# Pacing of embedding gathers: scratch writes between gathers replaced by an answered semaphore

## The reference

```python
h = relu(dense @ dw1 + db1)                      # 512 x 13 -> 512 x 64
dense_emb = relu(h @ dw2 + db2)                  # 512 x 64
sparse_emb = emb_tables[f_ids, sparse_idx]       # 512 x 26 x 64, tables 26 x 12500 x 64
emb = concatenate([dense_emb[:, None, :], sparse_emb], axis=1)
inter = einsum('bfd,bgd->bfg', emb, emb)         # 27 x 27 products per sample
pairs = inter[:, iu0, iu1]                       # the 351 above the diagonal
z = concatenate([emb.reshape(B, -1), pairs], axis=1)
z = relu(z @ ow1 + ob1)                          # 2079 -> 512
z = relu(z @ ow2 + ob2)                          # 512 -> 256
z = relu(z @ ow3 + ob3)                          # 256 -> 128
return z @ ow4 + ob4                             # 128 -> 1
```

## Time and profile before

| | |
|---|---|
| median of the runs | 188.66 us |
| the profiled execution, whole | 187.21 us |
| its span, first to last instruction | 185.4 us |
| TensorE busy, mean granted clock | 127.4 us (69%), 0.88 |
| GpSimd busy | 123.8 us (67%) |
| ScalarE, VectorE busy | 42.2 us, 37.8 us |
| gathers on GpSimd | 104, 98.9 us busy |
| scratch writes on GpSimd | 90, 24.7 us busy |

### The profile page before, as it was taken

How to read it: one execution, slowest core, us unless ns; L and a number is a source line. 1 busy time by engine, 2 the same in 40 slices (tenths; PEclk the granted TensorE clock), 3 DMA queues, 4 the chain that set the end, 5 groups by cost and what they waited for, 6 DMA issues and landing times.

```text
span 185.4 us, 3069 instructions
## 1 busy us (share of the span) xinstructions
PE 127.4 (69%) x1301; PEld 68.8 (37%) x1301; DVE 37.8 (20%) x97; ACT 42.2 (23%) x96; POOL 123.8 (67%) x199
## 2 busy tenths in 40 slices
PE   1510285828655995839439993959729979989994
PEld 0000132514344442524226432424426446656453
DVE  2700003000142204100144005000234023136011
ACT  0440310031046201040075001040174011166011
POOL 3888888888735888888565888888367887200000
PEclk9999999975965699996965798587997999999999
DMA  5999532221212332312312332222222324100000
GB/s 157 409 332 357 172 26 23 23 28 21 21 13 23 21 22 24 28 22 26 24 13 24 23 27 20 23 28 20 19 20 20 22 25 31 18 4 0 4 0 0
DMA packets 4576, 9.80 MB, mean 53 GB/s; under 512 B 2065, under 2 KB 2065, under 8 KB 3922
## 3 DMA queue, kind: packets, MB, share of 16 engines
q0 software_dynamic: 3328, 3.41, 21.3%
q1 hardware_dynamic: 1010, 5.30, 7.1%
q10 hardware_dynamic: 224, 0.89, 1.6%
HBM read 9.59 MB, written 0.00 MB: 52 GB/s over the span
## 4 chain that ended last, share of the span: by engine, by line
PE 45%; POOL 26%; issue 18%; ACT 5%; DMA 3%; DVE 2%
PE acc L259 20%; POOL gathered L211 20%; PE acc L292 10%; PE inter L276 7%; POOL pace L219 6%; PE acc L310 4%; DMA gathered<-tables,rows 2%; ACT emb L386 1%; ACT emb L387 1%; PE turned L240 1%; PE acc L301 1%; ACT pairs L392 1%; DMA idx_raw<-idx 1%; ACT z L399 1%; DVE emb L466 1%
## 5 line engine op out<-in xcount | busy, mean ns | idle before, releaser
L211 POOL DMA_INDIRECT gathered<-tables,rows x104 | 98.9, 951 | 34.6 <-issue 16.9
L259 PE MATMUL acc<-w,emb 128*128 128x512 f32 x104 | 65.7, 780 | 19.4 <-issue 12.3
L259 PEld LDWEIGHTS acc<-w,emb 128*128 128x128 f32 x104 | 31.3, 315 | 46.3 <-issue 36.9
L392 ACT ACTIVATE pairs<-inter 28x96 f32<-28x96 f32 (+1 forms) x64 | 15.7, 246 | 39.8 <-PE inter L276 39.1
L219 POOL MEMSET pace<- 128x192 uint8 x90 | 24.7, 274 | 0.1
L292 PE MATMUL acc<-w,pairs 128*128 128x512 f32 x56 | 24.7, 592 | 0.0
L182 DVE COPY pairs<-inter 28x96 f32<-28x96 f32 (+1 forms) x64 | 17.0, 266 | 26.5 <-PE inter L276 25.8
L276 PE MATMUL inter<-emb 64*28 64x28 f32 x1024 | 12.6, 204 | 13.8 <-DMA gathered<-tables,rows 10.1
L240 PE MATMUL turned<-small,gathered 128*128 128x128 f32 x52 | 10.1, 317 | 13.5 <-DMA gathered<-tables,rows 13.5
L386 ACT ACTIVATE emb<-turned 128x512 f32<-128x512 f32 x8 | 8.8, 1098 | 45.7 <-issue 28.6
L465 DVE COPY emb<-turned 128x512 f32<-128x512 f32 (+1 forms) x7 | 5.5, 784 | 64.1 <-issue 49.5
(11 more groups left out here) (47 smaller groups left out, 26.3 us busy)
## 6 DMA issues: line engine op xcount, KB each, us to landing
w<-w SPq DMA_DIRECT2D x5, 1024.0 KB, 8.7
gathered<-tables,rows POOLq DMA_INDIRECT x104, 3.4
small<-small_pack ACTq DMA_DIRECT2D x1, 706.5 KB, 6.0
dense_sb<-dense_pack ACTq DMA_DIRECT2D x1, 160.5 KB
idx_raw<-idx SPq DMA_DIRECT2D x1, 39.0 KB
idx_raw<-idx SPq DMA_DIRECT2D x1, 13.0 KB, 1.9
out<-y SPq DMA_DIRECT2D x1, 2.0 KB
```

The source lines that it names most:

```text
L211: pool.indirect_dma_start(out=gathered[:, t, s, :], out_offset=None, in_=tables, in_offset=bass.IndirectOffsetOnAxis(ap=rows[:, t, s:s + 1 ...
L259: nc.tensor.matmul(acc[t][:], emb[:, tile_of(t), place(2 * c)], w[:, c, :], start=(c == 0), stop=False)
L392: last = move(lambda dst, src: nc.scalar.activation(dst, src, ACT.Copy), t, k, (0, 1))
```

## The change

The scratch buffer and its writes are gone. Every gather now increments `gathers_issued`. SyncE waits for each gather's increment in turn and increments `echo` once (ECHOES = 1). GpSimd issues gather n = 26 t + s only when `echo` shows the answer to gather n - 2 (LAG = 2). The holds stay where they were, and TensorE waits for the same gathers as before, now counted on `gathers_issued`.

```diff
-PACE = 192
+ECHOES = 1
+LAG = 2
 HOLDS = [7, 10]
-UNPACED_FROM = 18
...
-        pace = sb("pace", [P, TILES * NF, PACE], mybir.dt.uint8)
...
-        gathers_held = sem("gathers_held")
+        gathers_issued = sem("gathers_issued")
+        echo = sem("echo")
...
                 sp.dma_start(w[:, groups, :], w1[:, groups, :]).then_inc(w_in[g], 16)
+            for n in range(TILES * NF - LAG):
+                sp.wait_ge(gathers_issued, n + 1)
+                for _ in range(ECHOES):
+                    sp.sem_inc(echo, 1)
             sp.wait_ge(y_done, 2)
...
                     for s in range(2 * c0, 2 * c1):
-                        held = t > 0 and s in HOLDS
+                        n = t * NF + s
+                        if n >= LAG:
+                            pool.wait_ge(echo, ECHOES * (n - LAG + 1))
                         pool.indirect_dma_start(
...
-                            engine_sem=gathers_held if held else None,
+                            engine_sem=gathers_issued,
                         ).then_inc(group_in[t][g], 16)
-                        if held:
+                        if t and s in HOLDS:
                             pool.wait_ge(inter_done, 2 * (t - 1) + HOLDS.index(s) + 1)
-                        elif t < LAST or s < UNPACED_FROM:
-                            nc.gpsimd.memset(pace[:, t * NF + s, :], 0)
...
                 if t < LAST:
-                    pe.wait_ge(gathers_held, 2 * t + k + 1)
+                    pe.wait_ge(gathers_issued, (t + 1) * NF + HOLDS[k] + 1)
```

## The result

The changed kernel took 221.67 us in the median of four runs (220.51 to 222.16), the kernel before 188.63 us (187.79 to 189.02). The ratio is 1.175, with a 95% interval of 1.169 to 1.181. I had forecast 183.1 us and a gain.

A forecast was written before the change was run, and what follows sets the result against it. Neither TensorE (69% busy) nor GpSimd (67%) was the bound by share; TensorE waited for gathers in places. Gains of 3.1, 0.28, 1.7, 0.28 and 0.28 made 5.6 us: 183.1 us against the 188.66 median, range 180.0 to 190.0.

The forecast's parts named there:

- My list of what would prove me wrong: Pitch above 1.35 us, gathers longer than 0.95, landings after 3.7, or TensorE's products lengthening by over 1.3 us a group.
- the clock: TensorE's granted clock: fewer waits may win or lose half-clock groups; taken as 0, with 2.5 us on each side.
- At most 3.7: Reading of the trace before: a gather takes 3.4 us from start to landing, at most 3.7.
- later than 3.7 us: Sign of being wrong: gathers that land later than 3.7 us after their start.
- Rival C: Every gather: the 0.27 us release adds to each 0.30 us gap, pitch 1.52, kernel slower at 199.1 us; chance 0.16.
- First tile: Up to interactions(0, 0): gathers come sooner, TensorE waits less, and its start moves from 50.62 to 47.5, 3.1 us.
- Hold: Hold of tile 1: the three gathers inside have two pitches of 0.14 us less, a gain of 0.28 us.
- Tile 1 with its hold: Tile 1: TensorE's waits of 0.81 and 0.88 us go, 1.7 us; the hold of tile 2 gives 0.28.
- Tile 2 with its hold: Tile 2: TensorE is already the later engine, GpSimd 1.1 us early, gain 0; the hold of tile 3 gives 0.28.
- Last tile: Last tile: field 25 already has 2.2 us of slack before turn(3, 3), so gain 0.
- case A: Whole kernel: the gain comes as summed, 183.1 us, own range 180.6 to 185.6; chance 0.60, 0.04 more for a gain beyond.

## Why the prediction was wrong

**The number failed on the chip of the result, and the step that failed was the one I didn't write as a step.** In the sum I let each copy start right behind its turn, as in the trace before, and counted only what gathers do to TensorE's waits for data. On that chip the increments behind four turns took 6 to 11 us, and one behind layer 2's products 4.3 us: 37 us of added waits where the sum had nothing. My list of what would prove me wrong has the pitch, the length of a gather, the landing and the clock, and not this. I took the trace of one execution as the behaviour of the kernel.

**One reading was too narrow as well.** "At most 3.7" for the landing covers only the 24 gathers whose landings were all recorded, each within eight gathers behind a hold. On chip 14, where all 104 are recorded, the same view gives, before and with the change:

```profile
DMA to landing us min/median/max: 2.3/3.3/7.3
DMA to landing us min/median/max: 2.3/3.3/6.9
```

The long ones are the first eleven gathers of tile 0 (4.2 to 7.3 us before), which run beside the weight loads. The median holds, so the sum doesn't change, but "later than 3.7 us" was no sign of being wrong.

**Rival C** had the right sign and the wrong mechanism. The wait is free. The pitch stays 1.25 us from the second gather to the 34th, so it was not the queue of GpSimd either. The Trainium skill, Advanced Engine Details and Errata, Engine Queue Depths, gives that queue eight places; in this trace nothing changes past the eighth gather. The warning of rival C, that only eight gathers in a row had been seen without a write, was right in one respect. What goes wrong in the result comes with long runs of them: turn(1, 1) and turn(2, 1), about 13 us into a run of gathers, are followed by copies that are 0.3 and 0.9 us late, and the four that are late by 6 us and more come over 20 us into one. The order isn't strict: turn(0, 0), which ends 17 us into the first run, is followed by its copy at once (20.74, 20.78).

**What is shown and what is not.** Shown: the changed kernel is 17.5% slower in the result's runs and about 5% faster on three chips. The difference is made by TensorE's increments, which reach the engines that wait for them up to 10.8 us late. On the chips of the experiments neither pitch, nor answers, nor about twice the increments makes it appear. Not shown: what is different about the result's chip, and whether the pitch or the answers do the harm there, since no variant ran on it. There are signs that something on it was busy before the change too. The kernel before was 2% slower there. Its landing events were incomplete in the trace. In its first interactions TensorE stood still twice, for 0.59 us before 51.69 and for 0.52 before 52.39, where on chip 14 the same 128 matmuls run through in 1.26 us:

```profile
51.69 0.18 PE L276 MATMUL inter<-emb 64*28 64x28 f32 x1 [0.59 <-issue]
```

One explanation that fits is a path for recorded events that is slow there, which gathers at 1.25 us fill, and which then holds up TensorE's increments but not those of GpSimd, SyncE and VectorE. A second one, not tested, is the recording itself: every run of the changed kernel on record is one that the profiler recorded, so it isn't shown that the kernel would be slow on that chip with nobody recording. Both are argued only: there is no run without a recorded trace and no second set of runs on that chip.

**On the other chips the steps of the sum can be checked**, with the two traces of chip 14. TensorE before:

```profile
50.47 1.26 PE L276 MATMUL inter<-emb 64*28 64x28 f32 x128 [0.59 <-DMA gathered<-tables,rows]
...
55.79 1.71 PE L276 MATMUL inter<-emb 64*28 64x28 f32 x128 [2.02 <-DMA gathered<-tables,rows]
...
73.89 6.54 PE L259 MATMUL acc<-w,emb 128*128 128x512 f32 x8 [2.43 <-DVE emb L466]
...
80.27 0.60 PE L240 MATMUL turned<-small,gathered 128*128 128x128 f32 x4
83.16 5.33 PE L259 MATMUL acc<-w,emb 128*128 128x512 f32 x8 [2.29 <-ACT emb L387]
...
90.66 1.27 PE L276 MATMUL inter<-emb 64*28 64x28 f32 x128
...
95.99 1.46 PE L276 MATMUL inter<-emb 64*28 64x28 f32 x128 [3.47 <-DMA gathered<-tables,rows]
...
129.35 1.26 PE L276 MATMUL inter<-emb 64*28 64x28 f32 x128 [2.41 <-DMA gathered<-tables,rows]
...
134.67 1.71 PE L276 MATMUL inter<-emb 64*28 64x28 f32 x128 [1.63 <-DMA gathered<-tables,rows]
```

and with the change:

```profile
28.38 0.60 PE L244 MATMUL turned<-small,gathered 128*128 128x128 f32 x4
31.41 3.79 PE L263 MATMUL acc<-w,emb 128*128 128x512 f32 x8 [2.43 <-DVE emb L470]
35.64 0.66 PE L244 MATMUL turned<-small,gathered 128*128 128x128 f32 x4 [0.44 <-DMA gathered<-tables,rows]
...
47.50 1.27 PE L280 MATMUL inter<-emb 64*28 64x28 f32 x128
...
52.56 1.71 PE L280 MATMUL inter<-emb 64*28 64x28 f32 x128 [3.19 <-DMA gathered<-tables,rows]
...
70.10 3.82 PE L263 MATMUL acc<-w,emb 128*128 128x512 f32 x8 [2.44 <-DVE emb L470]
...
76.88 3.82 PE L263 MATMUL acc<-w,emb 128*128 128x512 f32 x8 [2.29 <-ACT emb L391]
...
88.15 1.71 PE L280 MATMUL inter<-emb 64*28 64x28 f32 x128 [1.62 <-DMA gathered<-tables,rows]
...
119.20 1.27 PE L280 MATMUL inter<-emb 64*28 64x28 f32 x128
...
124.25 1.71 PE L280 MATMUL inter<-emb 64*28 64x28 f32 x128 [2.66 <-DMA gathered<-tables,rows]
```

- *First tile*: interactions(0, 0) from 50.47 to 47.50, 2.97 us; forecast 3.1, and a start at 47.5. Turn(0, 2) starts at 35.64, forecast 36.3. The held gather is done at 44.77 + 0.94 = 45.71, forecast 45.9, so TensorE is the later engine here, as forecast.
- *Hold*: 3.23 - 2.97 = 0.26 us; forecast 0.28.
- *Tile 1 with its hold*: the gain grows from 3.23 to 95.99 - 88.15 = 7.84, by 4.6 us; forecast 2.0. Of this, 1.7 us were for waits of 0.81 and 0.88 us for gathers, and in this trace before they don't exist: turn(1, 2) at 80.27 and interactions(1, 0) at 90.66 start without one. What gave most of the 4.6 us is the clock, which I had put at 0 with 2.5 either way, and that term is mis-sized here. Two groups of eight products take 3.82 us each instead of 6.54 and 5.33, 4.2 us less. The rows of tile 1 by stretch (clock third from last) show 0.77 before and 0.93 after:

```profile
57.40:90.60 33.20, 26.90 (x62) 12.16 (x53) 5.67 (x13) 4.76 (x11) 27.85 (x45) 0.77 0.28 23
```

```profile
54.20:83.10 28.90, 22.42 (x60) 11.78 (x54) 5.67 (x13) 4.75 (x11) 21.68 (x23) 0.93 0.30 26
```

- *Tile 2 with its hold*: by 2.6 us more, to 10.42; forecast 0.3. On this chip TensorE waited 2.41 us for the held gather at 129.35, so GpSimd was the later engine; in the trace that I forecast from it was the earlier by 1.1. The term rested on one execution in which the two engines were nearly level.
- *Last tile*: 0.4 us more, to the 10.8 between the spans of 183.6 and 172.8; forecast 0.

So on these chips case A has the right sign, 9 us in the medians (184.8 to about 175.5) where I had 5.6. The first tile and the hold came as summed; that is a third of the gain. The rest came from the clock and from which engine was the later one in tile 2, and neither was in the sum. The direction of the clock was the one that the Trainium skill, TensorE: Matmul & The Clock Gate, Part 1, gives for a busier array. By that rule the term should have been counted as a gain. In the mean these traces agree: TensorE is busy 69% of the span before and 71% after, at a granted clock of 0.888 and 0.911, and over all runs on chip 14 it is 0.879 to 0.907 before and 0.903 to 0.922 for the changed kernel. In the result's trace it went the other way, 0.828 after 0.880, as TensorE waited more.

## What to carry to other kernels

A gap between gathers may be worth more than the time it fills, and a trace of one chip doesn't show whether it is. Before taking out something that looks like a pause, run the kernel without it on several chips. Ask of every hand-over whether its latency may change with the load, the copy behind a transpose as much as the landing of a transfer, and give that a place among the rivals. Where two engines are level within a microsecond, forecast the tile from several executions, or carry both cases.

## What had not been expected of the hardware

The same program took 221.7 us in the result and 173.3 to 178.0 us on three other chips (other by inference, see above), while the kernel before differed by only 2% (188.6 and 184.4 to 185.6). In the result, TensorE's increments reached waiting engines up to 10.8 us late in and behind long runs of gathers, those of GpSimd, SyncE and VectorE did not, and one came to ScalarE at 51.39, 5.6 us after the last gather had left GpSimd (44.82 + 0.95). A wait that is already met, folded in front of a gather, costs nothing (gap 0.30 us with and without it). An increment by SyncE costs 0.06 us, and a scratch write of 4 bytes instead of 192 costs 0.12 us of GpSimd but 0.01 us of pitch.
